# Attention edges: the scans of the destination terms in pieces of 224 places, and the last group in two pieces

## The reference

```
feat = (h @ W).reshape(n, H, F)
el = jnp.sum(feat * al[None], axis=-1)
er = jnp.sum(feat * ar[None], axis=-1)
e = jax.nn.leaky_relu(el[src] + er[dst], NEG_SLOPE)
m = jax.ops.segment_max(e, dst, num_segments=n)
ex = jnp.exp(e - m[dst])
denom = jax.ops.segment_sum(ex, dst, num_segments=n)
a = ex / denom[dst]
msg = feat[src] * a[:, :, None]
out = jax.ops.segment_sum(msg, dst, num_segments=n)
...
h = gat_layer(h, src, dst, W1, al1, ar1, b1)
h = gat_layer(h, src, dst, W2, al2, ar2, b2)
```

## Time and profile before

| | |
|---|---|
| median of three runs | 7239.95 us |
| span of the profiled execution, first to last instruction | 7227.0 us |
| DVE busy | 5489.4 us (76%) |
| POOL busy | 5224.6 us (72%) |
| PE busy | 2303.9 us (32%) |
| gathers L1781 | 3126, 952 ns each |
| scans L1915 | 8, 3.45 us each |
| first `gat_edges`, first gather to the next stage's load | 2811.04 to 4794.65 us |
| second one | 5082.41 to 7067.12 us |

### The profile page before, as it was taken

How to read it: one execution, slowest core, us unless ns; L and a number is a source line. 1 busy time by engine, 2 the same in 40 slices (tenths; PEclk the granted TensorE clock), 3 DMA queues, 4 the chain that set the end, 5 groups by cost and what they waited for, 6 DMA issues and landing times. The chain is left out here.

```text
span 7227.0 us, 61561 instructions
## 1 busy us (share of the span) xinstructions
PE 2303.9 (32%) x10543; PEld 1547.9 (21%) x10543; DVE 5489.4 (76%) x9603; ACT 2205.4 (31%) x5460; POOL 5224.6 (72%) x5323
## 2 busy tenths in 40 slices
PE   4688888888888573000000000026000000000000
PEld 3455555555555463000000000014000000000000
DVE  7799999999999576666666666674567676666678
ACT  2688888888888341000000000011000000000001
POOL 4677777777776536777777777767777777777775
PEclk8899999999999797555555555558555555555555
DMA  7666676666766567676767676754566676767677
GB/s 229 191 204 203 204 204 204 203 205 202 206 203 194 140 162 184 208 222 208 223 208 223 207 224 207 223 162 102 176 211 219 211 221 209 221 208 223 209 228 235
DMA packets 821966, 1467.60 MB, mean 203 GB/s; under 512 B 215801, under 2 KB 552574, under 8 KB 821372
## 3 DMA queue, kind: packets, MB, share of 16 engines
q0 software_dynamic: 250192, 671.13, 34.9%
q1 hardware_dynamic: 571692, 795.57, 32.3%
HBM read 754.20 MB, written 713.36 MB: 203 GB/s over the span
## 5 line engine op out<-in xcount | busy, mean ns | idle before, releaser
L1781 POOL DMA_INDIRECT gb_g<-table,ix_g x3126 | 2974.8, 952 | 954.8 <-issue 950.3
L666 POOL DMA_INDIRECT gb<-table,ix x1563 | 1615.8, 1034 | 495.1 <-issue 471.2
L1887 DVE SCALAR_TENSOR_TENSOR gb_g<-gb_g,same_g,wv 128x256 f32<-128x256 f32 x3020 | 1447.9, 479 | 94.2
L1051 PE MATMUL pm<-ident,tl 128*4 128x128 f32 x2 | 0.7, 373 | 4013.3 <-DMA tl<-sums 4013.3
L1814 ACT ACTIVATE ww<-ee 128x132 f32<-128x132 f32 (+5 forms) x106 | 29.2, 276 | 3646.1 <-DVE ee L1865 3646.1
L1875 DVE TENSOR_TENSOR wv<-gb_g,ww 128x1024 f32<-128x1024 f32 (+1 forms) x784 | 955.1, 1218 | 0.0
L697 PE MATMUL po<-msg,sel 128*128 128x256 f32 x3144 | 857.4, 420 | 145.5 <-DVE msg L809 141.1
L1051 PEld LDWEIGHTS pm<-ident,tl 128*4 128x4 f32 x2 | 0.2, 82 | 4014.2 <-DMA tl<-sums 4014.2
L1857 DVE TENSOR_TENSOR ee<-gb_g,held 128x128 f32<-128x128 f32 (+5 forms) x106 | 38.5, 363 | 1073.9 <-DMA gb_g<-table,ix_g 1073.9
L697 PEld LDWEIGHTS po<-msg,sel 128*128 128x128 f32 x3144 | 613.5, 205 | 380.7 <-DVE msg L809 240.9
L689 PE MATMUL pt<-m,r 64*128 64x256 f32 x3136 | 462.1, 413 | 228.3 <-DVE msg L850 225.1
(11 more groups left out here) (291 smaller groups left out, 4354.0 us busy)
## 6 DMA issues: line engine op xcount, KB each, us to landing
sums<-gb_g SPq DMA_DIRECT2D x780, 528.0 KB, 3.5
sums<-ost SPq DMA_DIRECT2D x393, 512.0 KB, 3.2
gb_g<-table,ix_g POOLq DMA_INDIRECT x3126, 3.1
gb<-table,ix POOLq DMA_INDIRECT x1563
table<-f SPq DMA_DIRECT2D x48, 520.0 KB, 7.4
x<-in_x SPq DMA_DIRECT2D x50, 256.0 KB, 4.1
at<-in_rbf SPq DMA_DIRECT2D x100, 128.0 KB
hT_d<-hT SPq DMA_DIRECT2D x49, 256.0 KB, 3.7
```

Of the source, the lines that this page charges most:

```text
L666: eng.indirect_dma_start(out=gb[:, g, j, :, :].rearrange("p a c -> p (a c)"), out_offset=None, in_=q.table0[:, :], in_offset=bass.Indirect ...
L1781: eng.indirect_dma_start(out=gb[:, p, j, 0:FR], out_offset=None, in_=q.table1[:, :], in_offset=bass.IndirectOffsetOnAxis(ap=ix[:, p, j:j + ...
L1887: ins = eng.scalar_tensor_tensor(rows[:, t0 + t, 0:D], row, same[:, t:t + 1], wv[k % 2][:, j, :], ALU.mult, ALU.add)
```

## The change

Two edits, both for `gat_edges`. The first: each of the four scans of 1563 places becomes seven, six of 224 places and one of 219. The pieces go place by place, and in each all four heads. A piece that is not the first begins with the last value of its head's previous piece, and waits for it by the count of `s_held`; what waited for 4 scans (VectorE itself and GpSimd's `free`) now waits for 28. The second: the last group is cut into 15 and 12 tiles and no longer into 12, 8, 5 and 2, so that `ENDS` has four pieces and not six.

```
-ENDS = [(SB - 2, 0, 16), (SB - 2, 16, SBT)] + [(SB - 1, t, min(t + m, LAST)) for t, m in ((0, 12), (12, 8), (20, 5), (25, 7)) if t < LAST]
+ENDS = [(SB - 2, 0, 16), (SB - 2, 16, SBT)] + [(SB - 1, t, min(t + m, LAST)) for t, m in ((0, 15), (15, 17)) if t < LAST]
...
+    SPAN = 224
+    SPANS = -(-CE // SPAN)
...
                 def free(s, i, p):
                     if p == B - 1:
-                        eng.wait_ge(s_held, H)
+                        eng.wait_ge(s_held, H * SPANS)
...
-                for h in range(H):
-                    ins = eng.tensor_tensor_scan(held[:, h, :], q.samep[:, 0:CE], ch.rearrange("p (e h) -> p e h", h=H)[:, :, h], ini[:, h:h + 1], ALU.mult, ALU.add)
-                    ins.then_inc(s_held, 1)
-                eng.wait_ge(s_held, H)
+                for x, e0 in enumerate(range(0, CE, SPAN)):
+                    es = slice(e0, min(e0 + SPAN, CE))
+                    for h in range(H):
+                        first = ini[:, h:h + 1] if x == 0 else held[:, h, e0 - 1:e0]
+                        if x > 0:
+                            eng.wait_ge(s_held, (x - 1) * H + h + 1)
+                        eng.tensor_tensor_scan(held[:, h, es], q.samep[:, es], ch.rearrange("p (e h) -> p e h", h=H)[:, es, h], first, ALU.mult, ALU.add).then_inc(s_held, 1)
+                eng.wait_ge(s_held, H * SPANS)
```

## The result

| | before | after |
|---|---|---|
| median, us (9 runs each) | 7241.84 | 7224.37 |
| lowest and highest | 7236.85, 7247.45 | 7208.48, 7227.34 |
| span of the profiled execution | 7227.0 | 7206.3 |

The ratio is 0.9972, with a 95% interval of 0.9963 to 0.9982: 17.5 us faster, between 13 and 27. The forecast was 7223.0 and 17.0 us.

A forecast was written before the change was run, and what follows sets the result against it. GpSimd's gather issue was taken to bound the two edge stages. Scans 14.8 plus tail 2.2 gave 17.0 us off the 7227.0 span, 7210.0; with 12.95 us over the span, 7223.0, range 7215 to 7232.

The forecast's parts named there:

- What bounds: In the two attention-edge stages, GpSimd's gathers set the pace, one per 1.25 us; VectorE has about 11 us idle per group.
- How a gather is caught: At the stage's start, a gather starting inside a two-input scan waits for its end, then needs 0.75 us.
- The pieces' length: Scans at the stage's start: 0.63 us per 224-place piece, one every 0.55 us, 15.5 us a layer.
- The beat: Gathers beside the scan pieces: two take 2.75 us where free ones take 2.50, 1.4 us late a layer.
- The bad beat: Rival, scans: nearly every gather caught late, 3.4 us a layer, and no tail gain; 7229.2 us; chance 0.14.
- The tail: Stage's end: last sum 3.1 us earlier, last store 2.0 later; net 1.1 us gained per layer, 2.2 for both.
- A sign of being wrong that came: For the edge stages: the forecast falls if the gathers' whole stretch shortens by less than 5 us a layer.
- Rival two: Scans: a gather keeps the lock throughout, so pieces stand still; 9.2 us lost a layer, only tail left; 7238; chance 0.06.
- Rival three: Scans: GpSimd does not get in between pieces, a gather waits out the chain; slower than before, 7249; chance 0.04.
- The sum: Whole kernel: 14.8 us from the scans and 2.2 from the tail, 17.0 us, giving 7223.0.

The follow-up runs named there:

- all runs of usual pace but the last: The last: against the kernel before, the change with 782-place scans, flags in PSUM, early last signal, `ep` in PSUM and `mm_` in SBUF; 7210.0 us, 0.9964.
- the runs with flags in PSUM: The change with 782-place pieces, `samep` copied to PSUM by ScalarE; 7204.9 against 7230.6 us before. Also with early last signal: 7219.4 against 7240.1.
- The separate runs: Against the kernel before: only the scans in pieces of 224, 7215.2 against 7230.6 us; only the last group in 15 and 12 tiles, 7235.5 against 7240.1.
- the first set: Four runs beside the kernel before at 8601.3 us: scans alone 8581.7, ends alone 8602.2, pieces of 248 places 8587.0, of 391 places 8606.8.
- the third set: Four runs beside the kernel before at 7240.1 us: ends alone 7235.5, 248 places 7219.1, PSUM flags with early signal 7219.4, short scans too 7210.0.

## Why the prediction was right, step by step

- **What bounds.** Right: the gathers' issue sets the pace, and VectorE's idle time hides 2.6 us of longer scans (16.2 for 13.6).
- **How a gather is caught.** Right: it needs 0.75 us from the end of the scan, with scans of 0.71, 1.0 and 1.8 us too. Incomplete in one point: a gather that starts in a scan's first 0.04 us is not caught. Then it is the scan that gets longer, 0.51 us for 0.44, as in the kernel before:

```profile
3022.37 0.51 DVE L1861 TENSOR_TENSOR_SCAN fs<-seg_add,ee 128x132 f32<-128x132 f32 x1
3022.40 0.95 POOL L1781 DMA_INDIRECT gb_g<-table,ix_g  x1 [0.30 <-issue]
```

- **The pieces' length.** Mis-sized. I took 0.63 us a piece, from a line through the earlier trace rows; it is 0.658. Two sizes of the same scan, 3.448 us for 1563 and 0.658 for 224, give 2.084 ns a place and 0.19 us fixed. The 132-place scan of L1861, another scan, has only 0.17 fixed, and the line was drawn through it. A layer's scans took 16.2 us, just over the 15 to 16 expected. The overlap of 0.08 was right.
- **The beat.** Right in kind: short and long gathers in turn. Mis-sized: 2.0 and 2.2 us late and not 1.4, because the long one takes 1.32 us and not 1.2, and two gathers need five pieces, 5 x 0.576 = 2.88 us. Wrong: "any distance from 0.53 to 0.60 is good". Four pieces are 2.304 us, and the long gather of the pair comes at 2.30, so it just misses that boundary; and one that has 0.09 us left may miss too. The bad beat, given 0.14, did come in one layer of one run, and cost 3.7 us, over its bound of 3.4.
- **The tail.** The mechanism was right, the sum low: 1.7 and 2.0 us gained, not 1.1. The last gather landed and was read 3.8 and 3.9 us after its start, not 4.2. The 11.8 us of work and 4.46 us to the load are each within 0.12 us of what was worked out (11.9 and 2.58 + 2.0). The second layer's old tail was 0.3 longer than the first's, which I had not counted.
- **What I did not see.** The short scans of the groups catch gathers as well: 1.0 to 3.8 us a layer over all runs of usual pace but the last, depending on where the gathers fall. In the profiled pair this hid 2.5 us of the gain. The earlier trace rows showed the effect, and I used it only to measure the lock.
- **A sign of being wrong that came.** The prediction was to fall if the gathers' whole stretch shortened by less than 5 us a layer. In the profiled pair, first gather's start to last gather's start, it shortened by 4.0 us in the first layer and 5.6 in the second. The scans gave their 6.4 and 7.0; the short scans and the plain gather took the rest back.
- **Rival two, the lock kept for a whole gather,** is out: pieces are never 0.9 us long (662 ns at most, 684 the first). The Trainium skill, "SBUF — State Buffer", section "SBUF: two separate sides", says that whichever of the two starts first has the pair for its whole instruction. For the scan as the holder the runs agree; for the gather they don't: a scan met by a gather's start is 0.08 us longer at most, and the gather takes 0.95. That a second SBUF input is what contends with a GpSimd instruction that reads SBUF, as the same section says, the runs with flags in PSUM bear out: 24 gathers at 0.95 us where 16 of 18 took 1.43 or more.
- **Rival three, no way in between the pieces,** is out for pieces of 224 places or more, at the first boundary. The 75-place pieces did once keep a gather out for two boundaries in each of two runs.
- **The sum** came out at 17.5 for 17.0, but in part by luck. In the two stages of the profiled pair only 13.3 us are found; scans 1.5 us short of their 14.8 and a tail 1.5 over its 2.2 cancel, and the 2.5 us of the short scans stood in no term. No row shows where the other 4 us of the medians come from; they are within the interval. The separate runs, 15.4 and 4.6 us, add up to 20.0, within their intervals. The 12.95 us that the sum added to the span were no fixed part: after the change the median is 18.1 us over the profiled span.

## What to carry to other kernels

Where GpSimd's indirect gathers set the pace, give VectorE's instructions beside them at most one SBUF input: put the other in PSUM, by an idle engine if need be. Here that removed the stall whole. Cutting the scans into pieces only turned it into a beat between two periods, which has to be worked out and which can flip from one run to the next. (Moving an input was tried with scans alone; that other instructions with two inputs in SBUF hold a gather too is read from rows, below.) Cut the end of such a stage so that the last piece starts when its last input lands, and don't let two stores wait for the same last signal.

## What the runs showed of the hardware

- A gather that starts 0.09 us before the boundary between two scans gets in at one time (0.95 us) and misses it at another (1.42 us). What decides is not settled.
- The second SBUF input holds gathers in other instructions as well. In the first set 119 gathers began inside the `tensor_tensor` that adds `gb_g` and `held`, both in SBUF (0.38 us, L1859 after the change), behind its first 0.04 us and with over 0.20 us of it left. All were late, 0.98 to 1.11 us, and ended 0.77 to 0.78 us after it, as here:

```profile
8095.47 0.38 DVE L1859 TENSOR_TENSOR ee<-gb_g,held 128x128 f32<-128x128 f32 x1
8095.53 1.10 POOL L1783 DMA_INDIRECT gb_g<-table,ix_g  x1 [0.30 <-issue]
```

  Of the 13267 that began, in all profiles, inside the instructions with one such tensor in SBUF and one in PSUM (`gb_g` with `ww` or `wv`, L1875 and L1887 before), as far into them and with over 0.25 us left, none took more than 0.97 us.
- A gather and a two-input scan that start within some 0.04 us of each other both go on: the gather takes 0.95 us, and the scan 0.44 to 0.52 us where it takes 0.44 alone.
- The same kernel before took 7240.1 us in one set and 8601.3 us in another, at 203 GB/s over the span; a variant of it beside the slow one had 171 GB/s, and its gathers waited 575 us for buffers. Why that set was slow is not known.
- A plain gather took 945.2 to 945.6 ns in nine of the fourteen profiles and 948.1 to 948.5 in five: all four of the third set and one of the first. With 3126 of them this is 9 us, more than some of the edits give: times and spans of different sets are not to be compared.
